# A fused FFN, attention, FFN kernel: rows normalised by halves, the last output by blocks, and a new table of step times

## The reference

```python
x = x + 0.5 * ffn(layernorm(x))
x = x + attention(layernorm(x))
x = x + 0.5 * ffn(layernorm(x))
# ffn: h = silu(x@w1.T*s1) * (x@w2.T*s2); h = gelu(h@h1.T*s); h = gelu(h@h2.T*s); h@w3.T*s3
# w1, w2: 1024x256; h1, h2: 1024x1024; w3: 256x1024, all with entries -1, 0, 1
# attention: 16 heads; row n looks at rows n-o for 24 fixed offsets o, softmax over the 24,
#            times sigmoid(x@Wgate+b), then @Wout
```

## Time and profile before

| | |
|---|---|
| three runs | 1532.97, 1529.48, 1532.85 us, median 1532.85 |
| the profiled execution | 1529.28 us, of which the span of the trace is 1527.4 |
| TensorE busy, share of the span | 96% |
| DVE, ACT, POOL busy | 67%, 44%, 37% |
| mean granted TensorE clock | 0.994 |
| traffic in the first of 40 slices (38.2 us) | 297 GB/s |

### The profile page before, as it was taken

One profiled execution on the slowest core, in us unless ns is written; L12 is line 12 of the kernel. 1 busy time (PEld: TensorE's weight loads), 2 busy tenths in 40 slices (PEclk: granted clock), 3 DMA queues, 4 the chain that ended last, 5 costly groups with the idle time before them and its releaser, 6 DMA issues.

```text
span 1527.4 us, 19080 instructions
## 1 busy us (share of the span) xinstructions
PE 1472.4 (96%) x6914; PEld 1207.8 (79%) x6914; DVE 1025.6 (67%) x1349; ACT 679.3 (44%) x1063; POOL 572.1 (37%) x466
## 2 busy tenths in 40 slices
PE   6989999999999999999899999899999999989998
PEld 5777878787877788878687878788888878778887
DVE  6524777875867677859684978596577777872322
ACT  7653545343535344444353534435344444343532
POOL 3011263462462436251735170807225345353100
PEclk9999999999999999999999999999999999999999
DMA  8765668766575775858656777585675867854332
GB/s 297 274 244 172 208 215 319 245 236 214 193 258 180 253 275 188 279 173 288 234 182 209 264 243 249 186 288 177 218 251 179 287 226 235 285 194 145 103 118 71
DMA packets 189347, 338.21 MB, mean 221 GB/s; under 512 B 15680, under 2 KB 138688, under 8 KB 188864
## 3 DMA queue, kind: packets, MB, share of 16 engines
q1 hardware_dynamic: 189248, 336.93, 64.4%
HBM read 314.85 MB, written 30.41 MB: 226 GB/s over the span
## 4 chain that ended last, share of the span: by engine, by line
PE 83%; POOL 5%; DVE 4%; DMA 3%; ACT 3%; issue 2%; SPq 0%; DVEq 0%; POOLq 0%; ACTq 0%
PE f_bank L1155 27%; PE f_bank L1156 27%; PE a_banks L1230 7%; PE f_bank L1115 6%; PE f_bank L1116 6%; PE f_bank L1184 3%; PE f_bank L1185 3%; PE a_banks L1250 2%; POOL acc L773 2%; DMA weights_hi<-in_ffn_w 2%; DVE slot L1026 1%; DMA slot<-keys_and_values 1%; POOL h_lo L787 1%; PE f_bank L1103 1%; DVE slot L1070 1%
## 5 line engine op out<-in xcount | busy, mean ns | idle before, releaser
L1155 PE MATMUL f_bank<-h_hi,wring 128*128 128x512 f32 x2048 | 810.9, 396 | 8.0 <-DMA wring<-weights_hi 3.8
L1156 PE MATMUL f_bank<-h_lo,wring 128*128 128x512 f32 x2048 | 799.6, 390 | 0.0
L1155 PEld LDWEIGHTS f_bank<-h_hi,wring 128*128 128x128 f32 x2048 | 385.6, 188 | 92.1 <-DVE h_lo L926 4.7
L1156 PEld LDWEIGHTS f_bank<-h_lo,wring 128*128 128x128 f32 x2048 | 385.8, 188 | 80.9 <-issue 2.2
L856 ACT ACTIVATE h_hi<-f_bank,colv 128x512 fp32r<-128x512 f32 x256 | 176.4, 689 | 544.5 <-PE f_bank L1156 544.2
L926 DVE TENSOR_TENSOR h_lo<-f_bank,h_hi 128x512 fp32r<-128x512 f32 x256 | 175.8, 687 | 250.2 <-ACT f_bank L857 249.1
L787 POOL TENSOR_TENSOR h_lo<-f_gated,h_hi 128x512 fp32r<-128x512 f32 x128 | 170.3, 1343 | 348.0 <-ACT h_hi L850 347.5
L1115 PE MATMUL f_bank<-fT_hi,w_in 128*128 128x512 f32 x512 | 205.8, 402 | 9.2 <-ACT f_gated L845 3.8
L1116 PE MATMUL f_bank<-fT_lo,w_in 128*128 128x512 f32 x512 | 200.9, 392 | 0.0
L1026 DVE TENSOR_TENSOR slot<-slot,a_banks 128x1280 f32<-128x1280 f32 (+4 forms) x124 | 170.6, 1376 | 16.3 <-DMA slot<-keys_and_values 16.2
L1032 DVE TENSOR_REDUCE S<-slot 128x80 f32<-128x1280 f32 (+4 forms) x124 | 171.7, 1385 | 4.3
(11 more groups left out here) (115 smaller groups left out, 1141.4 us busy)
## 6 DMA issues: line engine op xcount, KB each, us to landing
wring<-weights_hi SPq DMA_DIRECT2D x248, 512.0 KB, 4.8
slot<-keys_and_values SPq DMA_DIRECT2D x128, 384.0 KB, 4.6
slot<-keys_and_values SPq DMA_DIRECT2D x64, 640.0 KB, 4.3
slot<-keys_and_values SPq DMA_DIRECT2D x312, 128.0 KB, 4.5
slot<-keys_and_values SPq DMA_DIRECT2D x64, 256.0 KB, 5.6
weights_hi<-in_ffn_w SPq DMA_DIRECT2D x16, 512.0 KB, 6.8
keys_and_values<-kv_out SPq DMA_DIRECT2D x32, 256.0 KB, 3.2
slot<-in_ffn_w SPq DMA_DIRECT2D x10, 512.0 KB, 5.3
```

The source lines that it names most:

```text
L1155: pe.matmul(bank[:, :], hi, h_hi[src][:, k, :], start=(k == 0), stop=False)
L1156: last = pe.matmul(bank[:, :], hi, h_lo[src][:, k, :], start=False, stop=(not general and k == KH - 1))
```

## The change

1. A pass's input is normalised in two halves of two row blocks: `f_stats`, `f_rstd` and `f_scale` are each issued twice with half the columns. F0's rows are loaded by two DMAs of 256 KB on two semaphores, instead of one of 512 KB.
2. The first `f_in` of a pass waits for `fT_hi` before its two matmuls with the high part, and for `fT_lo` only after them; the four matmuls of that bank are reordered from high, low, high, low to high, high, low, low (so in all `f_in` steps).
3. In the last pass each of the four output blocks of 256 columns has a bank of its own, a residual of its own and a store of its own (128 KB).
4. The tables `TIMES`, `FOLLOW`, `OPENING` and `STARTS` have new values, and with them the order of steps on every engine.

```diff
-TIMES = [3.65, 9.56, 11.46, 12.91, 17.19, 25.44, 22.37, 3.94, 7.13, 53.75, 61.23, 3.2, 93.09, 4.73]
+TIMES = [3.25, 9.27, 11.97, 11.99, 17.77, 25.46, 22.37, 3.94, 7.12, 53.75, 61.23, 3.2, 93.09, 5.62]
-FOLLOW = dict(silu=-1.5, gate=-0.08, cut=1.63, low=1.99, gelu=-0.77,
-              lo=1.12, residual=-0.87, store=2.93, fill=23.53, stats=-0.47, turn=4)
+FOLLOW = dict(silu=-1.58, gate=-0.08, cut=1.75, low=2.02, gelu=-0.77,
+              lo=1.05, residual=-0.88, store=4.45, fill=28.68, stats=-0.89, turn=4)
-OPENING = dict(block=9.27, block_step=1.86, compare=2.04, turn=8.2, input=13.0, count=52.85)
-STARTS = [50.0, 118.7, 184.3, 274.4, 343.7, 411.3, 489.6, 575.0,
-          642.8, 722.6, 789.0, 867.0, 962.9, 1038.6, 1110.1, 1179.0]
+OPENING = dict(block=6.77, block_step=1.86, compare=2.07, turn=7.35, half=1.39, input=12.12, count=50.05)
+STARTS = [50.0, 118.7, 182.2, 274.4, 343.9, 411.3, 490.9, 575.2,
+          643.4, 722.6, 789.0, 864.5, 963.0, 1038.0, 1110.2, 1178.4]
...
-                            steps += [(now, "f_stats", (following,)), (now + 3, "f_rstd", (following,)),
-                                      (now + 5, "f_scale", (following,))]
+                            for bp in range(2):
+                                now = done + FOLLOW["stats"] + 1.5 * bp
+                                steps += [(now, "f_stats", (following, bp)), (now + 1.8, "f_rstd", (following, bp)),
+                                          (now + 3.7, "f_scale", (following, bp))]
...
             for n in range(OB):
-                out_half(passes[-1], n)
+                for block in range(2):
+                    done = pe([3.54, 1.88, 0.23, 1.88][2 * n + block], "f_out", r, n, block)
+                    steps += [(done + 0.2, "f_residual", (r, n, block)), (done + 1.2, "f_store", (r, n, block))]
...
-            steps = [(4.0, "f_stats", (FIRST,)), (6.5, "f_rstd", (FIRST,)), (8.6, "f_scale", (FIRST,))]
+            steps = []
             for bp in range(2):
-                here = at["turn"] + 0.5 * bp
-                steps += [(here, "f_turn", (FIRST, bp)), (here + 0.7, "f_evict", (FIRST, bp)), (here + 1.5, "f_tlo", (FIRST, bp))]
+                here = at["turn"] + at["half"] * bp
+                steps += [(here - 4, "f_stats", (FIRST, bp)), (here - 2.8, "f_rstd", (FIRST, bp)),
+                          (here - 1.1, "f_scale", (FIRST, bp)), (here, "f_turn", (FIRST, bp)),
+                          (here + 0.7, "f_evict", (FIRST, bp)), (here + 1.5, "f_tlo", (FIRST, bp))]
...
-                sp.dma_start(xf[:, r.p, :, :], src).then_inc(f_loaded[r.p], 16)
+                if r is not FIRST:
+                    sp.dma_start(xf[:, r.p, :, :], src).then_inc(f_loaded[r.p], 16)
+                for bp in range(2 if r is FIRST else 0):
+                    half = slice(2 * bp, 2 * bp + 2)
+                    sp.dma_start(xf[:, r.p, half, :], src[:, half, :]).then_inc(x_half if bp else f_loaded[r.p], 16)
...
                 if m == 0:
-                    pe.wait_ge(f_tlo, r.at(2, 2))
+                    pe.wait_ge(f_thi, r.at(2, 2))
...
                         pe.matmul(bank[:, :], w12(m, w, k), fT_hi[:, k, :], start=(k == 0), stop=False)
+                    if (m, w) == (0, 0):
+
+                        pe.wait_ge(f_tlo, r.at(2, 2))
+                    for k in range(KD):
                         last = pe.matmul(bank[:, :], w12(m, w, k), fT_lo[:, k, :], start=False,
                                          stop=(lo is None and k == KD - 1))
```

More of the change, by code:

```diff
@@ L726, in _ @@
                 for n in range(2):
-                    sp.wait_ge(f_stored[p][n], 16 * TILES)
+                    sp.wait_ge(f_stored[p][n], 16 * TILES + (16 if p == passes[-1].p else 0))
                 sp.wait_ge(a_stored[p], 16 * TILES)
@@ L799, in _, with f_scale @@
         def _(act):
-            def f_scale(r):
-                act.wait_ge(f_rstd, r.at(1, 1))
-                for i in range(NB):
+            def f_scale(r, bp):
+                act.wait_ge(f_rstd, r.at(2, bp + 1))
+                for i in range(2 * bp, 2 * bp + 2):
                     last = act.activation(f_hat[:, i, :], xf[:, r.p, i, :], ACT.Identity,
                                           bias=f_shift[:, i:i + 1], scale=f_rs[:, i:i + 1])
-                    if i % 2:
-                        last.then_inc(f_norm, 1)
+                last.then_inc(f_norm, 1)
             def a_hat_(a):
@@ L1171, in run_hidden, with run_out, part @@
                     part(1, EARLY, KH)
[L1173 to L1174 removed]
+            def run_out(r, n, block, ring, general):
+                blocks = ring.of_step(key("f_out", r, n) if block is None else key("f_out", r, n, 0))
                 for i in blocks:
                     pe.wait_ge(s_ring[i % 4], ring.filled(i))
[L1178 to L1188 removed]
+                def part(half, at, first, stop):
+                    for k in range(first, stop):
+                        to = f_bank("f_out", r, half)[:, at * D:(at + 1) * D] if block is None else                             f_bank("f_out", r, half, at)[:, 0:D]
+                        t = slice((2 * half + at) * P, (2 * half + at + 1) * P)
+                        w = w_out3[:, k // 4, (k % 4) * D:(k % 4 + 1) * D]
+                        pe.wait_ge(r.marks.lo, r.of("lo", KH + k + 1))
+                        pe.matmul(to, h_hi[r.p][:, k, t], w, start=(k == 0), stop=False)
+                        last = pe.matmul(to, h_lo[r.p][:, k, t], w, start=False, stop=(not general and k == KH - 1))
+                        if general:
+                            w_lo = wring[:, blocks[k // 4] % 4, (k % 4) * D:(k % 4 + 1) * D]
+                            last = pe.matmul(to, h_hi[r.p][:, k, t], w_lo, start=False, stop=(k == KH - 1))
@@ L1189, in part @@
                     return last
                 ahead = KH - 1 if r.last and not general else 0
-                for half in range(n, OB) if ahead and n == 0 else [n] if not ahead else []:
-                    bank_free(int(general), *key("f_out", r, half))
-                    for k in range(ahead):
-                        part(half, 0, k)
-                for k in range(ahead, KH):
-                    part(n, 0, k)
-                for k in range(KH):
-                    last = part(n, 1, k)
+                if block is None:
+                    bank_free(int(general), *key("f_out", r, n))
+                    part(n, 0, 0, KH)
+                    last = part(n, 1, 0, KH)
+                elif block == 0:
+                    for half in range(OB) if ahead and n == 0 else [n] if not ahead else []:
+                        bank_free(int(general), *key("f_out", r, half, 0))
+                        if ahead:
+                            part(half, 0, 0, ahead)
+                    last = part(n, 0, ahead, KH)
+                else:
+                    bank_free(int(general), *key("f_out", r, n, 1))
+                    last = part(n, 1, 0, KH)
```

80 lines of the change are left out of this document (39 added, 41 removed).

## The result

The changed kernel takes 1517.31 us, median of six runs (1515.01 to 1522.36), against 1530.63 before (1528.38 to 1532.97, six runs): ratio 0.992, 95% interval 0.9903 to 0.9938. The profiled executions, 1517.73 and 1529.28 us, differ by 11.55. Beside the earlier trace rows, the busy times have hardly moved, but for POOL's 17.6 us more in 64 more instructions.

A forecast was written before the change was run, and what follows sets the result against it. TensorE, busy 96% of the span, bounds the kernel; its late start, end, waits and low clock can be won. Opening -1.4, end -0.7, reordering with A8 -5.35 give -7.45: median 1532.85 becomes 1525.4 us, range 1519 to 1534.

The forecast's parts named there:

- the charge of 8 x 0.43 = 3.5 us for moved steps: Eight moved TensorE steps (A2, A7, z turns of A10, A11, A14) each charged the mean wait: cost 3.5 us, bounds 0 and 9.
- the fills: Weight fills for the first four hidden steps go out 5 us earlier on SP; none is late now, so no gain.
- the halves of F1 to F15: Normalising 15 later passes by halves: 1.3 us more POOL work per pass, 19 us in all, hidden except at A8.
- The opening: Kernel start: half the rows land earlier, first `f_in` at about 12.45 instead of 13.88; gain 1.4 us, bounds 0 and 1.9.
- The rival of an unchanged opening: Opening doesn't start earlier, as ACT waits for weights or half loads finish together: 1526.8 us; chance 0.13.
- The end: Last pass's output: residual 0.6 us shorter, last store 0.1 less; gain 0.7 us, bounds 0.2 and 1.1.
- A11: Starts 2.5 us earlier in the plan: `a_turn` waits 1.6 instead of 2.24 us, kv0 loses 1.50; gain 3.8, bounds 0 and 5.4.
- Covered waits: Steps put between TensorE neighbours at A0, A1, A6, and `a_z_turn` of A6 moved back: gain 3.25 us, bounds 0 and 3.25.
- A8: Half of F8's normalisation goes ahead of `a_rstd` and `a_hat`, so kv0 starts 1.1 us later: cost 1.1, bounds 0 and 2.8.
- F14: POOL's `a_add` of A15 starts 1.2 us earlier, first hidden step waits 1.8 instead of 3.02: gain 2.9, bounds 0 and 4.7.
- Rival one: The reordering nets nothing, new waits cost what old ones cost, only the two ends gain: 1530.75 us; chance 0.32.
- Rival two: POOL becomes late, the slower side; chance 0.10.

The follow-up runs named there:

- `fill` alone: The kernel before with one number changed, fills of weights due 28.68 instead of 23.53 us ahead of their step: 1531.0 us, ratio 0.9999.

## Why the prediction came out too small, point by point

The change was forecast at 7.45 us and measured at 13.3. In the time itself the miss is larger, 1517.31 for 1525.4, since I had started from 1532.85, the median of three runs, and six give 1530.63: 2.2 of the 8.1 us are that base. From 1530.63 the same range would begin at 1516.8, so the time would lie just inside it; that is the luck of three runs and says nothing for the sum. The step that failed is the charge of 8 x 0.43 = 3.5 us for moved steps: at the five sub-tiles there is no new wait in the changed kernel. Two terms that I had put at nothing, the fills and the halves of F1 to F15, and the two ends, which were mis-sized, come next.

- **The opening, forecast 1.4 us, measured 2.26 at the first `f_in`.** The chain went step by step as written. The term that was mis-sized is the landing of the half: 3.57 instead of 4.25, beyond my bound of 0.9 us for 256 KB; I had divided by the mean traffic of the first 38 us, and at the start 256 KB took 1.16. The rival of an unchanged opening is refuted.
- **The end, forecast 0.7, measured 1.47.** The residual was right (0.54 for 0.6). The store was taken at 0.1 us less, and is 0.9 less between the two profiles and 0.6 between the means of all (4.25 us behind the residual against 3.62), so the part is worth 1.2 rather than 1.47.
- **A11, forecast 3.8, measured 4.28.** Wait 1.64 for 1.6, kv0's wait gone, clock 1.00: right. But it isn't a gain of this number alone. The step that let me count it whole was a comparison of the two complete orders, which was the right way to do it.
- **Covered waits, forecast 3.25, measured about 1.** A0's 0.78 gave 0.96. A1's 0.69 is gone, but F2's layer 1 is no shorter (+0.08). At A6 a wait of 0.73 for `a_hat` took the place of 0.69 for `aT`, and F6 as a whole gained nothing. The wait of 1.09 for `z` of A6 is gone, and F7's layer 0 is 0.14 us shorter in one profile, 1.77 in the other. F2's second layer to F5 lost 0.5 in other places.
- **The fills, forecast nothing, measured 1.8 us in F2.** I asked only whether a fill is late. In the old order one 512 KB fill goes out just ahead of the four gathers on which A1's first `a_score` waits, and one among them (not both between them, as I had written for that experiment). In the kernel before, SP, DVE and TensorE:

```profile
203.59 0.47 SPq L710 DMA_DIRECT2D wring<-weights_hi  x1
205.62 1.33 SPq L677 DMA_DIRECT2D slot<-keys_and_values  x3
207.00 0.47 SPq L710 DMA_DIRECT2D wring<-weights_hi  x1
207.58 1.54 SPq L677 DMA_DIRECT2D slot<-keys_and_values  x1
```
```profile
212.40 1.49 DVE L1026 TENSOR_TENSOR slot<-slot,a_banks 128x1280 f32<-128x1280 f32 x1 [1.97 <-DMA slot<-keys_and_values]
```
```profile
216.72 0.66 PE L1240 MATMUL a_banks<-ident,z 128*128 128x128 f32 x4 [1.56 <-DVE z L1076]
```

  The `a_score` waits 1.97 us here, 0.25 to 1.99 in seven other profiles with the old value, and 0 in all ten profiles with the new one. `z` of A0 stands behind it. With `fill` alone F2 gains 1.82 against the first profile of before and 0.72 against the second, so a part of the 1.8 is that profile's luck. What a transfer is queued ahead of had to be asked, too.
- **A8, forecast +1.1, measured +1.0 and +1.8.** The mechanism is as written (both waits, kv0 a microsecond later), but its size stays open: the layer is 0.98 longer without the halves too, and 0.76 in the second profile of before. That the halves cost nothing elsewhere was right, but they gain 0.8 us or a little more at F2 and at F9, and I had no term for that.
- **F14, forecast 2.9, measured 0.9 and 2.1.** The wait was 1.99 + 0.26 for 1.8. The terms for A11 and F14 also hold 1.7 us of lower clock each, 10 us at 0.83 instead of 1.00. That a wait costs this, from about 2.5 us on, was my estimate, and no run shows it as a fixed price: in F14 the clock from 1360 to 1370 us was 0.83 in one profile of the changed kernel and 1.00 in the next, with nearly the same waits, and at A11 two profiles of before have 0.83 and 0.73 from 980 to 990 us.
- **The charge of 3.5 us for eight moved steps.** This is the step that failed most. Of the places that I had named, A7, A10 and A14 have no new wait in either profile of the changed kernel, and A2 keeps one of 0.25 (0.23 before). A mean over all steps of a kind is the price of a place chosen at random; the kernels with one table or one number changed show that such places do exist (5.5 us at A6, 2.49 at `z` of A14, 1.77 at `z` of A10), and that the two tables together avoid them. The rows couldn't tell that, but the two POOL orders could: for A6, a step that newly stands behind an `a_add` of 5 us can be listed without the chip. That such a list would have found all of them was not tried.

Summed against forecast: charge 3.5 too much, fills 1.8, opening and end 1.6, halves 1.7 and A11 0.5 too little, against 2.3 for the covered waits and 0.8 to 2 for F14 too much; what is left over is of the size of the layers' chance. Rival one, the reordering nets nothing, is refuted by the tables' 11.5 us. Rival two, POOL late by the halves' extra work, is refuted by the kernel without them in F1 to F15, which is slower and not faster; a late `a_rstd` did cost 7 us with one start changed, but there it was the order and not the extra work. The step of 3.6 us between the runs of before is now explained in part: F0's layer 1 and F8 each move by 2 to 4 us with the landing of transfers.

## What to carry to other kernels

Where orders come from due times, compare the complete sorted lists of every engine and look for short steps with a waiting consumer that newly stand behind a long one: 1.3 us in one number cost 6 to 7 us here, and two tables that each lose 6 us gained 7 together, so an edit of such tables can't be priced or tested number by number. Profile the unchanged kernel twice before trusting differences of a few microseconds, since one late transfer moved a layer by up to 4.4 us. Then take the largest remaining wait, name the step it is queued behind, swap the two, and look at the next consumer, which may get a part of the wait.

## What the runs showed of the hardware

- The granted clock after a wait isn't fixed by its length alone. With a wait of 2.40 us at `a_turn` of A5 it was 1.00 before and 0.84 in the changed kernel, both from 500 to 510 us. In F14 two profiles of the changed kernel have waits of 1.99 + 0.26 and 1.97 + 0.50 us, with 0.83 and with this:

```profile
1360.00:1370.00 10.00, 7.53 (x33) 5.92 (x33) 4.31 (x5) 2.48 (x4) 9.71 (x6) 1.00 0.45 158
```

- Halving the last store from 256 to 128 KB saved 0.6 us of the time from the last residual to the end of the span (between means of ten and eight profiles), while 128 KB at the 353 GB/s of the changed kernel's busiest slice would be 0.4 us.
- A power of two columns instead of four takes 0.71 instead of 1.04 us on POOL, as in the earlier trace rows; the three small steps around it take 0.2 us in either size, so the halves cost 16.8 of the 17.6 us by which POOL is busier, as against 19 forecast.
